# Attention and mixture of experts in one kernel: expert output moved beside the projections, halves made at projection, features regrouped by DMA

## The chip, the cores and the metric

The kernel runs on one core of a Trainium2 chip. The metric is the device time of one execution in microseconds. The time before is the median of three runs.

## The reference, cut to what matters

Input x is 4 x 1024 tokens of 256 values, all fp32. xn is the layernorm of x over its last dimension; the result is x + attention(xn) + experts(xn).

```
Q, K, V = (xn @ W.T).reshape(16, 4, 1024, 16)      # a plain reshape, not a transpose
scores  = einsum('hbqd,hbkd->hbqk', Q, K)
out     = einsum('hbqk,hbkd->hbqd', softmax(scores), V).reshape(b, s, -1)
y = out + xn;  attention = (y - mean(y)) / sqrt(var(y) + eps)      # over a whole batch entry
gates = two largest of xn @ w_gate.T (8 experts), softmax over the two
experts = sum over e of gates[:, e] * ((xn @ w_in[e].T) @ w_out[e].T)
```

The reshape cuts the 4096 tokens into 64 groups of 64 tokens (n = 0 to 63). Each group is one attention problem of 1024 positions of 16 values. As an expert has no nonlinearity, w_in[e].T @ w_out[e].T is first multiplied to one 256 x 256 matrix, its composite.

## The kernel before, in words

Products are made from fp32r values, which hold only the upper part of a number, so most operands are kept as two halves: hi, the cast value, and lo, the rest. A projection or an expert product is three products (hi x hi, hi x lo, lo x hi) summed in PSUM. The order on every engine is written out by hand, with semaphores between the engines; SP, ACT and POOL each run their lists in order. SP and ACT also issue the DMAs.

Stage one goes over eight chunks of 512 tokens (four tiles of 128). For chunk c, DVE and POOL make the layernorm (`layernorm`, L597 to L615), TensorE transposes it (L838), ACT copies hi (L456) and DVE makes lo (L626). TensorE projects query and key (`project_qk`, L849) and values with gate logits (`project_v`, L860), and makes the composite of expert c+1 in two halves of its weights (`expert_product`, L871); ACT and DVE cut the composite into halves (L446, L633). ACT copies query and key to `stage` and stores them to DRAM (`qk_d`), and values to `v_d`; the transposed halves go to DRAM as well (`xt_store`). SP loads x and, in two slots (`wp`), the weights (`load_weights`, L272, L274).

Stage two has two parts side by side. TensorE makes expert output tile by tile (`y_bank`, L907: four PSUM banks, each with two experts, six products each) from transposed halves that SP loads back from DRAM (`next_xt`), and DVE multiplies by the gates and adds (`add_experts`, L708, L710, L714). Meanwhile ACT loads query and key from `qk_d` regrouped to [16 values, 1024 positions] per group (`load_qk`, L518), casts hi (L525), POOL subtracts lo (L396), and ACT stores three rows of halves for queries and three for keys to `feat_d` (`split_qk`, L529).

The last eight tiles of 32 go beside the first sixteen turns of maxima: a turn is a block of 128 query positions of group 0 or 1 against 1024 keys (`max_scores`, L936) and its maximum on DVE (`maxima`, L725). In turn 10 the maxima of group 0 are transposed (`maxima_to_rows`, L980); they come through POOL (`max_halves`, L405, L407). SP puts them as two further rows into the query features (`max_rows`, L329).

The attention loop then goes over n: `scores` (L948, 50 rows: 48 of halves and two of the maximum), exponentials on ACT (`exps`, L557), the sum over values (L959) and, for group n+2, the maxima. SP loads the features of group n+4 (`features`, L314, four loads), values and maxima rows of group n+1. A normalisation over batch entries and the stores of the result end the kernel.

## Time and profile before

| | us |
|---|---|
| median of 3 runs (lowest, highest) | 1100.63 (1099.38, 1101.2) |
| profiled execution: time, span | 1102.04, 1100.2 |
| busy: TensorE matmul, VectorE | 999.7 (91%), 846.7 (77%) |
| busy: ScalarE, POOL | 648.6 (59%), 117.2 (11%) |
| mean granted TensorE clock | 0.96 of full |
| DMA | 133.59 MB in 115766 packets, 47328 of them under 512 B |

A profile is of one execution. The busy time of TensorE is that of its matmul row, in which pipelined products overlap, so a busy TensorE isn't one at its peak. A row gives the line of the kernel, the engine, the tiles (written <- read) and a duration. SPq and ACTq are DMA issues on those queues. The 40 slices are of 27.5 us each.

### The profile page before, as it was taken

Reading aid. Unit: us, or ns where it says so; the run is one execution under the profiler, and the core shown is the slowest. Engines: PE = TensorE matmul, PEld = TensorE weight load, DVE = VectorE, ACT = ScalarE, POOL = GpSimd, SP = SyncE. Lnnn points to the kernel's source line nnn. Section 1 sums busy time; section 2 is a strip of 40 time slices with the busy share of each in tenths; the row PEclk is TensorE's granted clock in tenths of the full one; section 3 lists DMA queues with packets and bytes.
Section 4 is the critical chain, followed back from the end, with each engine's and each line's share of the span. In section 5 each row is a group of like instructions: output and inputs, shape, how many; then the busy total and the mean of one; then the engine's idle time right before and its main releaser. Section 6 shows DMA issues by size and latency. Waiting matters only on the chain.

```text
span 1100.2 us, 21325 instructions
## 1 busy us (share of the span) xinstructions
PE 999.7 (91%) x7816; PEld 512.7 (47%) x7816; DVE 846.7 (77%) x1108; ACT 648.6 (59%) x1240; POOL 117.2 (11%) x221
## 2 busy tenths in 40 slices
PE   7999999999920699999999999999999999999995
PEld 6888878888710433333333333333333333333332
DVE  5333376767830479999999999999999999999976
ACT  3334310000000048888888888888888888888885
POOL 3221121011111100000000000000000000000001
PEclk9999999999965769999999999999999999999998
DMA  7999697679766512222223232322223232323214
GB/s 269 377 327 330 243 172 187 184 184 227 165 156 154 206 28 54 72 57 70 68 60 72 54 72 54 72 56 71 63 65 72 54 72 54 72 54 72 64 22 154
DMA packets 115766, 133.59 MB, mean 121 GB/s; under 512 B 47328, under 2 KB 84960, under 8 KB 115680
## 3 DMA queue, kind: packets, MB, share of 16 engines
q1 hardware_dynamic: 62560, 77.64, 27.2%
q10 hardware_dynamic: 53120, 54.80, 17.5%
q8 instruction: 55, 0.90, 0.4%
q14 instruction: 31, 0.25, 0.1%
HBM read 80.75 MB, written 50.59 MB: 119 GB/s over the span
## 4 chain that ended last, share of the span: by engine, by line
PE 69%; ACTq 9%; DMA 8%; ACT 5%; issue 5%; POOL 2%; DVE 1%; SPq 0%; POOLq 0%; DVEq 0%
PE ps L959 23%; PE ps L948 21%; PE ps L936 10%; DMA feat_d<-wp 8%; ACTq L529 5%; PE ps L871 4%; PE ps L849 4%; ACTq L518 4%; ACT wp L557 3%; PE ps L860 2%; PE ps L907 2%; PE ps L970 2%; ACT vstage L557 1%; PE ps L982 1%; POOL xnc L396 1%
## 5 line engine op out<-in xcount | busy, mean ns | idle before, releaser
L725 DVE TENSOR_REDUCE negm<-ps 128x1 f32<-128x1024 f32 x512 | 618.7, 1223 | 49.5 <-PE ps L936 40.7
L557 ACT ACTIVATE wp<-ps 128x512 f32<-128x512 f32 x684 | 374.0, 597 | 86.1 <-PE ps L948 62.6
L948 PE MATMUL ps<-qf,xth 50*128 50x512 f32 x1024 | 258.5, 499 | 23.3 <-ACT wp L557 13.8
L959 PE MATMUL ps<-wp,vb 128*17 128x256 f32 x2736 | 216.1, 388 | 0.1
L936 PE MATMUL ps<-xth,qf 48*128 48x512 f32 x1024 | 210.4, 403 | 0.3 <-DVE negm L725 0.3
L948 PEld LDWEIGHTS ps<-qf,xth 50*128 50x128 f32 x1024 | 98.3, 185 | 230.7 <-ACT wp L557 128.3
L557 ACT ACTIVATE vstage<-ps 128x512 f32<-128x512 f32 x170 | 101.7, 598 | 29.4 <-PE ps L948 17.8
L907 PE MATMUL ps<-mth,xtth 128*128 128x512 f32 x256 | 103.7, 405 | 1.0 <-ACT vstage L481 1.0
L936 PEld LDWEIGHTS ps<-xth,qf 48*128 48x128 f32 x1024 | 100.6, 190 | 8.5 <-issue 5.9
L959 PEld LDWEIGHTS ps<-wp,vb 128*17 128x17 f32 x2736 | 46.9, 95 | 118.6 <-ACT wp L557 46.1
L907 PE MATMUL ps<-mtl,xtth 128*128 128x512 f32 x256 | 101.8, 398 | 0.0
L907 PE MATMUL ps<-mth,xttl 128*128 128x512 f32 x256 | 101.8, 397 | 0.0
L557 ACT ACTIVATE picks<-ps 128x512 f32<-128x512 f32 x170 | 101.5, 597 | 0.0
L710 DVE SCALAR_TENSOR_TENSOR acc<-ps,gates,acc 128x256 f32 (+1 forms) x128 | 61.8, 483 | 43.3 <-PE ps L907 40.6
L525 ACT CAST wp<-stage 128x1024 fp32r<-128x1024 f32 x8 | 8.0, 1045 | 107.2 <-issue 107.2
L525 ACT CAST wp<-xnc 128x1024 fp32r<-128x1024 f32 x8 | 8.0, 1044 | 95.9 <-issue 95.9
L871 PE MATMUL ps<-wp 128*128 128x256 f32 x256 | 58.4, 387 | 5.7 <-DMA wp<-w_out_t 5.7
L907 PEld LDWEIGHTS ps<-mth,xtth 128*128 128x128 f32 x256 | 48.5, 189 | 15.9 <-issue 4.6
L405 POOL TENSOR_TENSOR mpart<-negm,zero 128x8 fp32r<-128x8 f32 x64 | 12.8, 200 | 402.1 <-DVE negm L725 402.1
L871 PEld LDWEIGHTS ps<-wp 128*128 128x128 f32 x256 | 49.1, 194 | 12.3 <-issue 5.7
L907 PEld LDWEIGHTS ps<-mth,xttl 128*128 128x128 f32 x256 | 48.5, 190 | 11.7
L959 PE MATMUL ps<-vstage,vb 128*17 128x256 f32 x680 | 53.7, 387 | 0.3 <-issue 0.2
(107 smaller groups left out, 775.8 us busy)
## 6 DMA issues: line engine op xcount, KB each, us to landing
qf<-feat_d SPq DMA_DIRECT2D x128, 192.0 KB, 3.4
feat_d<-wp ACTq DMA_DIRECT2D x32, 512.0 KB
xth<-feat_d SPq DMA_DIRECT2D x128, 96.0 KB, 3.4
wp<-w_in SPq DMA_DIRECT2D x16, 512.0 KB, 5.3
wp<-w_out_t SPq DMA_DIRECT2D x16, 512.0 KB, 6.3
qk_d<-stage ACTq DMA_DIRECT2D x8, 1024.0 KB, 5.1
v_d<-vstage ACTq DMA_DIRECT2D x8, 544.0 KB, 3.2
vb<-v_d SPq DMA_DIRECT2D x128, 34.0 KB, 2.1
```

Of the source, the lines that this page charges most:

```text
L518: act.dma_start(dqk[p][b * DH:(b + 1) * DH].rearrange("d (g t) -> d g t", t=TB), qk_d.rearrange("f (g d) t -> d (f g) t", d=DH) [:, :, bas ...
L529: act.dma_start(feat_d[f, bass.ds(c * BC, BC), r * DH:(r + 1) * DH, :], (hi[p][f].bitcast(FP32), dq[p][f])[part]).then_inc(feat_out[2 * p ...
L557: nc.scalar.activation(weight_tile(n, j, b)[:, h * HALF:(h + 1) * HALF], ps[:, ST_BANK[(2 * unit + b) % 3], :], ACT.Exp).then_inc(exp_done, 1)
L710: nc.vector.scalar_tensor_tensor(out=total, in0=product, scalar=gate, in1=total, op0=ALU.mult, op1=ALU.add).then_inc(ff_added[j], 1)
L725: nc.vector.tensor_reduce(negm[:, n % 2, qt:qt + 1], ps[:, b:b + 2, :].rearrange("p b c -> p (b c)"), AX.X, ALU.max, negate=True).then_inc ...
L849: last = nc.tensor.matmul(ps[:, QK_BANK[o], :], w[:, o // 2, kt, (o % 2) * P:(o % 2 + 1) * P], v[:, p, kt, :], start=i == 0, stop=i == len ...
L860: last = nc.tensor.matmul(ps[:, bank, 0:D + E], x_t[:, p, kt, t * P:(t + 1) * P], w[:, kt, :], start=i == 0, stop=i == len(products) - 1)
L871: last = nc.tensor.matmul(ps[:, M_BANK[dh], 0:D], win[s][:, h, dh * P:(dh + 1) * P], wout[s][:, h, :], start=s == 0 and h == 0, stop=s == ...
L907: last = nc.tensor.matmul(ps[:, Y_BANK[j], :], v[:, slot, kt, :], m[:, kt, 2 * j:2 * j + 2, :].rearrange("p e d -> p (e d)"), start=i == 0 ...
L936: last = nc.tensor.matmul(ps[:, MAX_BANK[turn % 2] + half, :], qf[rows, u, qt * P:(qt + 1) * P], kf[rows, u, :], start=True, stop=True)
L948: nc.tensor.matmul(ps[:, ST_BANK[(2 * unit + half) % 3], :], kf[rows, u, j * P:(j + 1) * P], qf[rows, u, h * HALF:(h + 1) * HALF], start=T ...
L959: last = nc.tensor.matmul(ps[32 * c:32 * c + VW, PV_BANK, 0:POS // 4], vb[:, n % 2, j + b * NKT // 2, :], weight_tile(n, j, b)[:, c * (POS ...
```

## The change

The order of the stages is changed and the query and key features take another way.

1. The composites of all eight experts are made first, beside chunk 0 alone. SP loads all weights through the same two slots and the eight chunks of x between them.
2. Then, for each chunk, TensorE makes the expert output of its four tiles directly from the transposed halves in SBUF, and between the tiles the transposes and projections of the next chunk. The store of the halves to DRAM and their loads go. The gate weights are computed chunk by chunk instead of once.
3. Query and key outputs are cut into halves when they leave PSUM: ACT copies hi, DVE subtracts to lo, and ACT stores each of four outputs of a chunk twice (eight stores of 256 KB on ACT's queue). `qk_d` now holds [16 column groups, query or key, hi or lo, 16, tokens].
4. `regroup`, eight DMAs a chunk on SP's queue, copies from `qk_d` to `feat_d` in DRAM, 256 KB each, in pieces of 64 tokens (256 B). `load_qk`, `split_qk` and POOL's split loop go. `feat_d` holds hi and lo once; `features` reads hi twice, in eight loads instead of four.
5. The last four tiles (before: eight) go beside the sixteen turns, one bank a turn. `kf` is a tile of its own, no longer laid over `xth`. Values and projections share two PSUM banks.

```diff
-    qk_d = nc.dram_tensor("qk_d", [2, KT * P, T], FP32, kind="Internal").ap()
-    feat_d = nc.dram_tensor("feat_d", [2, NB, FR, POS], FP32, kind="Internal").ap()
+    qk_d = nc.dram_tensor("qk_d", [G, 2, 2, DH, T], FP32, kind="Internal").ap()
+    feat_d = nc.dram_tensor("feat_d", [NB, 2, 2, DH, POS], FP32, kind="Internal").ap()
...
             for half in range(2):
                 first = half * ROWS
-                yield qf, slice(first, first + FR), slice(0, POS), feat_d[0, n]
-                yield kf, slice(first, first + FR), slice(0, HALF), feat_d[1, n, :, half * HALF:(half + 1) * HALF]
+                keys = slice(half * HALF, (half + 1) * HALF)
+                yield (qf, slice(first, first + 2 * DH), slice(0, POS),
+                       feat_d[n, 0, 0].unsqueeze(0).to_broadcast([2, DH, POS]))
+                yield qf, slice(first + 2 * DH, first + FR), slice(0, POS), feat_d[n, 0, 1]
+                yield kf, slice(first, first + 2 * DH), slice(0, HALF), feat_d[n, 1, :, :, keys]
+                yield kf, slice(first + 2 * DH, first + FR), slice(0, HALF), feat_d[n, 1, 0, :, keys]
...
+            def regroup(c):
+                for half in range(2):
+                    sp.wait_ge(qk_stored[half], 64 * (c + 1))
+                for n in range(BC * c, BC * (c + 1)):
+                    sp.dma_start(feat_d[n].rearrange("f h d (g t) -> (f h d) g t", t=TB),
+                                 qk_d[:, :, :, :, n * TB:(n + 1) * TB].rearrange("g f h d t -> (f h d) g t")
+                                 ).then_inc(regrouped[c], 16)
...
+            for e in range(1, E):
+                load_x(e)
                 for h in range(2):
-                    load_weights(2 * k - 1, h)
...
+                    load_weights(e, h)
...
+            regroup(0)
             sp.wait_ge(att_const, 2)
-            for f in range(2):
-                sp.wait_ge(feat_out[f], 48)
...
+            sp.wait_ge(regrouped[0], 16 * BC)
+            for n in range(SLOTS):
+                features(n)
+            sp.wait_ge(v_stored, 16)
+            values(0)
+            for c in range(1, NC):
+                regroup(c)
             sp.wait_ge(v_stored, 16 * NC)
-            values(0)
             max_rows(0)
...
                     for half in range(2):
                         sp.wait_ge(st_ready[half], NKT * (n + 1))
+                    if (n + SLOTS) % BC == 0:
+                        sp.wait_ge(regrouped[(n + SLOTS) // BC], 16 * BC)
                     features(n + SLOTS)
...
             def qk_out(c):
...
+                act.wait_ge(qk_stored[0], 64 * c)
                 for o in range(4):
...
+                    act.wait_ge(project_ready, 2 * TC * c + TC + o + 1)
+                    nc.scalar.copy(stage[:, o, :].bitcast(FP32R), ps[:, PROJECT_BANK[o % 2], :]).then_inc(qk_hi, 1)
+                    for half, (done, staged) in enumerate(((qk_hi, stage), (qk_lo, lo_stage))):
+                        act.wait_ge(done, 4 * c + o + 1)
+                        act.dma_start(qk_d[o % 2 * G // 2:(o % 2 + 1) * G // 2, o // 2, half, :, c * CH:(c + 1) * CH],
+                                      staged[:, o, :]).then_inc(qk_stored[half], 16)
...
+            for c in range(1, NC):
+                xt_out(c)
+                v_out(c)
+                second_weight(c)
                 qk_out(c)
...
+            def qk_lo_halves(c, outputs):
+                for half in range(2):
+                    dve.wait_ge(qk_stored[half], 64 * c)
+                for o in outputs:
+                    dve.wait_ge(qk_hi, 4 * c + o + 1)
+                    nc.vector.tensor_tensor(lo_stage[:, o, :], ps[:, PROJECT_BANK[o % 2], :], stage[:, o, :], ALU.subtract
+                                            ).then_inc(qk_lo, 1)
...
+            for c in range(NC - 1):
+                for i in range(TC):
+                    add_experts(TC * c + i, range(E // 2))
+                    if i == 0:
+                        lo_halves(c + 1)
+                    elif i == 1 and c + 2 < NC:
+                        layernorm(c + 2)
+                    elif i == 2:
+                        choose_experts(c + 1)
+                        qk_lo_halves(c + 1, range(2))
+                    elif i == 3:
+                        qk_lo_halves(c + 1, range(2, 4))
+                        gate_weights(c + 1)
+            for i in range(2 * NKT):
+                n, qt = divmod(i, NKT)
+                add_experts(NT - TC + i // 4, [i % 4])
...
                 maxima(n, qt)
...
+            for e in range(2, E):
+                for h in range(2):
+                    expert_product(e, h)
...
             pe.wait_ge(ml_done, KT * E)
...
+            for c in range(NC - 1):
+                for i in range(TC):
                     for j in range(E // 2):
-                        y_bank(XS * k + slot, slot, j)
+                        y_bank(TC * c + i, j)
+                    if i == 0:
+                        transposes(c + 1)
+                    elif i == 1:
+                        for t in range(TC):
+                            project_v(c + 1, t)
+                    else:
+                        for o in range(2 * i - 4, 2 * i - 2):
+                            project_qk(c + 1, o)
```

## Rows read from the trace of the kernel before

**Rows 1.** The page's 40 slices from 0: busy tenths, clock, GB/s

```profile
PE   7999999999920699999999999999999999999995
...
PEclk9999999999965769999999999999999999999998
...
GB/s 269 377 327 330 243 172 187 184 184 227 165 156 154 206 28 54 72 57 70 68 60 72 54 72 54 72 56 71 63 65 72 54 72 54 72 54 72 64 22 154
```

**Rows 2.** The page's chain of waits, shares of the span by line

```profile
PE ps L959 23%; PE ps L948 21%; PE ps L936 10%; DMA feat_d<-wp 8%; ACTq L529 5%; PE ps L871 4%; PE ps L849 4%; ACTq L518 4%; ACT wp L557 3%; PE ps L860 2%; PE ps L907 2%; PE ps L970 2%; ACT vstage L557 1%; PE ps L982 1%; POOL xnc L396 1%
```

**Rows 3.** The chain in order of time: start us, us, what

```profile
332.06 11.76 DMA feat_d<-wp
343.90 0.33 ACTq L518
```

**Rows 4.** Who waited for whom: us in total, times, longest us

```profile
PE ps L980 <- POOL mpart L407: 56.7, 1, 56.7
```

**Rows 5.** Timeline of TensorE: the first scores (start us, us, instruction)

```profile
391.05 0.69 PE L948 MATMUL ps<-qf,xth 50*128 50x512 f32 x2 [1.66 <-DVE ps L755]
```

**Rows 6.** Stretches: PE, PEld, DVE, ACT, POOL busy; clock, DMA share, GB/s

```profile
192.50:220.00 27.50, 27.50 (x119) 22.15 (x118) 19.75 (x45) 0.00 (x0) 1.44 (x1) 1.00 0.70 184
...
338.00:340.00 2.00, 0.00 (x0) 0.00 (x0) 0.00 (x0) 0.00 (x0) 0.00 (x0) 0.50 0.51 211
...
340.00:367.00 27.00, 0.00 (x0) 0.00 (x0) 0.00 (x0) 3.98 (x4) 9.53 (x6) 0.50 0.66 152
...
391.00:411.00 20.00, 19.14 (x97) 6.67 (x101) 13.23 (x13) 11.32 (x21) 0.80 (x4) 0.51 0.12 31
```

**Rows 7.** The chain in order of time, one chunk of stage one

```profile
33.92 5.58 PE ps L849 x24
39.49 1.47 PE ps L860 x12
40.96 0.87 PE ps L838 x8
...
43.30 6.91 PE ps L871 x32
```

**Rows 8.** DMA issues: count, KB each, median us to landing

```profile
wp<-w_out_t SPq DMA_DIRECT2D x16, 512.0 KB, 6.3
```

**Rows 9.** Timeline of VectorE in four stretches

```profile
17.12 1.39 DVE L597 BATCH_NORM_STATS2 st<-acc 128x6 f32<-128x256 f32 x4
...
20.75 1.38 DVE L615 TENSOR_SCALAR xnc<-acc,mean,rstd 128x256 f32<-128x256 f32 x4 [1.42 <-POOL rstd L381]
...
140.94 0.19 DVE L672 TENSOR_REDUCE top<-lg 128x4 f32<-128x32 f32 x1 [3.85 <-ACT lg L479]
...
143.41 0.19 DVE L685 TENSOR_TENSOR gap<-top 128x32 f32<-128x32 f32 x1
...
146.46 0.48 DVE L710 SCALAR_TENSOR_TENSOR acc<-ps,gates,acc 128x256 f32 x1 [0.39 <-DVE gates L692]
...
150.28 0.48 DVE L710 SCALAR_TENSOR_TENSOR acc<-ps,gates,acc 128x256 f32 x1
...
299.82 0.48 DVE L710 SCALAR_TENSOR_TENSOR acc<-ps,gates,acc 128x256 f32<-128x256 f32 x1 [0.17 <-PE ps L907]
...
301.84 0.49 DVE L710 SCALAR_TENSOR_TENSOR acc<-ps,gates,acc 128x256 f32<-128x256 f32 x1
```

**Rows 10.** Groups of instructions: busy us, mean ns of one, idle before

```profile
L469 ACT COPY stage<-ps 128x512 f32<-128x512 f32 x32 | 18.8, 587 | 27.6 <-PE ps L849 27.6
```

**Rows 11.** Timeline of SP's DMA issues in the attention loop

```profile
602.80 0.42 SPq L314 DMA_DIRECT2D xth<-feat_d  x1
607.20 1.18 SPq L319 DMA_DIRECT2D vb<-v_d  x2
```

**Rows 12.** DMA from 150 to 157 us, while qk_d's pieces are loaded

```profile
DMA packets 3723, 1.06 MB, mean 152 GB/s; under 512 B 3165, under 2 KB 3723, under 8 KB 3723
...
q10 hardware_dynamic: 3133, 0.78, 97.7%
```

More of the change, by code:

```diff
@@ L522, in split_qk @@
-            def split_qk(c, p, gen):
-                act.wait_ge(dq_in[p], 16 * BC * (gen + 1))
-                for f in range(2):
-                    nc.scalar.copy(hi[p][f], dq[p][f]).then_inc(hi_done[f], 1)
-                for f in range(2):
-                    act.wait_ge(lo_done[f], c + 1)
-                    for r, part in enumerate(((0, 0, 1), (0, 1, 0))[f]):
-                        act.dma_start(feat_d[f, bass.ds(c * BC, BC), r * DH:(r + 1) * DH, :],
-                                      (hi[p][f].bitcast(FP32), dq[p][f])[part]).then_inc(feat_out[2 * p + f], 16)
@@ L676, in pick, with choose_experts @@
                 g(nc.vector.tensor_tensor(onehot[:, rows], eq[:, rows], wide(first[:, rows]), ALU.is_equal))
-            for chunks, rows in ((NC - 1, slice(0, NT - TC)), (NC, slice(NT - TC, NT))):
-                for h in range(2):
-                    dve.wait_ge(lg_evac[h], 2 * chunks)
+            def choose_experts(c):
+                rows = slice(TC * c, TC * (c + 1))
+                dve.wait_ge(v_evac, 2 * TC * (c + 1))
                 pick(rows, lg, top1, oh1)
@@ L853, in project_v, with project_qk @@
-            def project_v(c, p, t):
-                bank = V_BANK[t % 2]
-                pe.wait_ge(v_evac[t % 2], 2 * c + t // 2)
-                pe.wait_ge(lg_evac[t % 2], 2 * c + t // 2)
+                    last.then_inc(xt_psum, 1)
+            def project_qk(c, o):
+                p = c % 2
+                if o < 2:
+                    pe.wait_ge(v_evac, 2 * (TC * c + o + 3))
+                else:
+                    pe.wait_ge(qk_lo, 4 * c + o - 1)
+                products = [(w, v, kt) for w, v in ((wqkh, xth), (wqkh, xtl), (wqkl, xth)) for kt in range(KT)]
+                for i, (w, v, kt) in enumerate(products):
+                    last = nc.tensor.matmul(ps[:, PROJECT_BANK[o % 2], :], w[:, o // 2, kt, (o % 2) * P:(o % 2 + 1) * P],
+                                            v[:, p, kt, :], start=i == 0, stop=i == len(products) - 1)
+                last.then_inc(project_ready, 1)
@@ L858, in project_v @@
+            def project_v(c, t):
+                p = c % 2
+                if t == 0:
+                    pe.wait_ge(xtl_done, KT * (c + 1))
+                if t >= 2:
+                    pe.wait_ge(v_evac, 2 * (TC * c + t - 1))
+                elif c:
+                    pe.wait_ge(qk_lo, 4 * (c - 1) + t + 3)
                 products = [(x_t, w, kt) for kt in range(KT) for x_t, w in ((xth, wvgh), (xth, wvgl), (xtl, wvgh))]
                 for i, (x_t, w, kt) in enumerate(products):
-                    last = nc.tensor.matmul(ps[:, bank, 0:D + E], x_t[:, p, kt, t * P:(t + 1) * P], w[:, kt, :],
+                    last = nc.tensor.matmul(ps[:, PROJECT_BANK[t % 2], 0:D + E], x_t[:, p, kt, t * P:(t + 1) * P], w[:, kt, :],
```

390 lines of the change are left out of this document (128 added, 262 removed).

## The prediction, before the changed kernel ran

> **What bounds the kernel now.** I read the 40 slices first [rows 1]. TensorE works in nearly all of them, except from slice 11 to 13, some 302 to 385 us, where it stands still and its clock falls. The chain of waits [rows 2] gives 8% of the span to the stores of the features and 9% to the DMA issues of the two lines around them (L529 and L518). In order of time [rows 3] a chunk of this work ends with the last of its six stores, issued at 332.06 and landed 11.76 us later, and only then are the loads of the next but one issued (343.90). Eight chunks run so, one behind the other, from the end of the projections to 367. The waits name the place where this is paid: TensorE's L980 (`maxima_to_rows`) stood for 56.7 us behind `mpart` [rows 4], whose POOL instruction stands behind the last subtraction of the split loop. So the order is: projections beside the experts' products to about 142 us, 24 token tiles of expert output and ten attention turns to 310 us, an idle hole to 367, six more turns, and the first scores at 391.05 [rows 5]. In the hole the granted clock is 0.50 of full (1.2 GHz) [rows 6]. After 391 everything is the attention loop, 709.2 us long.
>
> The profiled execution took 1102.04 us with a span of 1100.2, 1.84 around it. The median shown is 1100.63, 1.4 below that execution. I make the sum against the span and take the same distances.
>
> **Removed.** The 64 loads of `qk_d` into SBUF, 16 ScalarE casts, 16 POOL subtractions and 48 feature stores go, and with them the hole: 56.7 us. The round trip of x's halves through DRAM (16 stores, 64 loads) goes too; it was hidden behind TensorE, so it is worth nothing by itself.
>
> **First phase, composites alone.** Before, an expert's two halves (32 products, 6.91 us) lay between 9.4 us of other TensorE work, so that a chunk took 16.3 us and weights were in time [rows 7]. Now six experts follow each other with two weight slots. A slot's cycle is: 3.45 us of products (half of 6.91), two issues about 0.4 us apart, 6.3 us to landing of the second load [rows 8], some 0.3 us of semaphores: 10.5 us for an expert, where TensorE needs 6.9. Bandwidth isn't the limit (2.6 MB in 10.5 us is 250 GB/s, the slices reach 377). I start from before's first stretch, which is the same to 17 us (VectorE is at its second layernorm at 17.12 [rows 9]); these steps are estimates from the products' durations in [rows 7]: `project_v(0)` and expert 1's first half to 24, its second half, whose weights are asked for at 17, to 28. The four query and key outputs come next at ScalarE's pace, because for each it copies (0.59 [rows 10]), waits for VectorE's half (about as long) and issues two stores (0.42 each, as SP's in [rows 11]): some 2 us an output, to 36. Expert 2 to 43, experts 3 to 7 at 10.5: 95.5. TensorE stands for 3.5 us in each cycle, and a stand of 1.7 us ahead of the first scores was already followed by 20 us at 0.51 [rows 5, 6]. I charge 1.3 us for each of five restarts, and 1 for the last subtraction: **the chunks begin at 103 us**. The bounds: 85 if loads land in 4.5 us, 118 if every restart costs a half product at the low clock.
>
> **Seven chunks.** TensorE: four tiles of expert output, 24 products each; 119 products in 27.5 us [rows 6] are 0.231 each, so 5.55 a tile, 22.2 together; query and key 5.58, values 2 x 1.47, transposes 0.87 [rows 7]: 31.6 us. VectorE: four tiles at 3.8 us when nothing holds it up (146.46 to 150.28), a layernorm of 5.0 (17.12 to 22.13), twelve steps of the expert choice at 0.225 (140.94 to 143.41), gate weights about 1.4, `lo_halves` 1.3, query and key halves 2.6 [rows 9]: 28.2 us. So TensorE sets the pace, with 3.4 us to spare for VectorE. VectorE also waits on ScalarE's hi copies, whose next copy stands behind two store issues: some 2 us. I stepped through one chunk: VectorE is furthest behind at the chunk's end, 3.7 us after TensorE, and has caught up in the second tile. The four banks of the output always come free in time. I take 32.2 us, seven times is 225: **328 us**. ScalarE is busy some 12 us of the 32 with copies and issues and is no bound. POOL's one copy of `xn` a chunk (2 us) can block a sum of two SBUF operands, and falls in the same slack.
>
> **Sixteen turns with the last four tiles.** Each now has one bank and one maximum: VectorE takes 2.02 (299.82 to 301.84) [rows 9] and 0.5 more once a tile, TensorE 1.39 + 0.43. VectorE bounds: 34.3 us, plus the 3.7 by which it begins late and 0.7 for memset and first rows. Before, the corresponding sixteen turns held two banks at 3.42. `mpart` is free on POOL now, so no hole. **First scores at 367 us**, instead of 391.05 [rows 5]: 24 us earlier.
>
> **The attention loop.** Same engine work, 709.2 us. SP issues eight feature loads instead of four, with the same bytes: +4 x 0.46 = 1.9 us, in a stretch from 603.22 to 607.20 in which it only waits [rows 11], so nothing; without this cover `max_rows`, next in its queue, would start late and scores(n+1) wait for it. The load of query's two equal copies has a source whose outermost dimension is 2. The feature stores, with an outermost dimension of 8, kept 0.51 of the sixteen engines busy at 211 GB/s [rows 6], 26 GB/s for each of eight. If such a shape sets how many engines serve, two serve each copy: 128 KB take 2.5 us, twice per n: 5 us, over before `max_rows` is issued some 7 us after the first of the features. Cost 0, and up to 0.5 us per n if it is more (d). The 8 us that the low clock cost from 391 to 411 I leave in: it may go (-8) or stay.
>
> **The queues, the cost with no row.** `regroup` moves 8192 pieces of 256 B a chunk from DRAM to DRAM on SP's queue. Nearest row: 3723 packets, nearly all of 256 B, in 7 us with the engines full [rows 12]: 16 x 7 us / 3723 = 30 ns each. That is a read into SBUF; here the write is short too. From below 30 ns or 15.4 us a chunk, from above twice that, 31 us, each side paid in full. I take 35 ns (18 us), nearer the row, as reads and writes overlap. The split stores of query and key (outermost 8: half the engines, 2 MB at 211 GB/s) add 10 us on those engines and values 2: 30 us in a chunk of 32. It hides, and features are wanted only from n = 4 on. But `max_rows(0)` stands behind all eight regroups.
>
> **Sum.** 367 + 709.2 + 1.8 = 1078 for such an execution, 1.4 less for the median: **1076.6 us**, a gain of 24: 56.7 of hole and about 3 of low clock after it, less some 30 for weights and restarts, less 5 for VectorE's lateness.
>
> **Rivals.**
> (a) *Regroup backs up; slower.* `max_rows(0)` must land before 367. Regroups start at about 92; each of seven chunks costs the busier engines 512 packets plus 12 us, the last 512 packets alone: 92 + 84 + 4096 t = 367 gives t = 46 ns. Below that nothing; at 60 ns the last lands at 422, scores(0) waits 55 us and the median is 1131. For: the engines are near full already and short writes are new; the chain of before shows such pieces as slow. Against: 30 ns measured. The Trainium skill ("DMA: Bandwidth & Descriptors", "Specifications") states that transfers below 512 B make the engine read, modify and write; no row here shows a short write to DRAM, and by the Trainium skill alone this rival would win. Chance 17%.
> (b) *VectorE sets the chunk.* If its waits on ScalarE and POOL's port cost 7 us a chunk instead of 3, a chunk is 35.5: +23 us, 1100, no change. For: 28 of 32 us busy and a queue in strict order; against: each wait was stepped through. 8%.
> (c) *The low clock stays through the composites.* A half then takes 6.9 instead of 3.45, a slot's cycle 14; six times 3.5, less the 6.5 charged, is 14.5 us, up to 20 if loads are late too: median 1091 to 1097, still faster. For: every cycle has its stand; against: the products before it raised the clock each time. 15%.
> (d) *Two-engine loads hold up `max_rows` in every n.* If the key copies run on two engines as well, 8 us of each 10.5 are taken; 0.5 us per n times 60 is 30 us: 1107. For: 0.51 of the engines in [rows 6]; against: the key copies lie in DRAM with one step and may count as 32 rows. The Trainium skill ("DMA: Bandwidth & Descriptors", the rules for kernel authors, "Use all 16 engines") states that a leading broadcast of c copies confines a DMA to at most c engines; the share in [rows 6] agrees for 8, and by the Trainium skill two engines carry the query copies for certain. Chance 5%.
> (e) *No low clock at the start of attention and quick weights*: 1060. 12%. The forecast itself has 43%.
>
> **Numbers.** A measurement of this kernel tells 0.2%, 2.2 us. Faster: forecast, (c) and (e), with part of (b): 0.74. Same 0.05. Slower: (a), (d), a little of (b): 0.21. The range runs from 1058 to 1116, with part of (a)'s middle and all of (b) to (e); the likeliest case alone is 1068 to 1086.
>
> **What would show it.** The first tile of expert output at 103; chunks of 32.2 with TensorE at 9 throughout; the slices from 0 to 100 us with TensorE at 6 or 7 and perhaps a clock below 10; no wait of L980 on `mpart`; first scores at 367; 709 us from there. Wrong would be: TensorE waiting for `ff_added` or `qk_lo` in the chunks (b), a long wait of the first scores with DMA full to that point (a), a DMA wait of the scores in every n (d), `qf<-feat_d` landing in over 10 us.

## The result, and the profile after

The changed kernel takes **1067.18 us** (median of four runs, 1065.44 to 1068.25), the kernel before in the same session 1100.51: a ratio of 0.9697 with a 95% interval of 0.968 to 0.9714, 33 us faster. Forecast were 1076.6 us in a range of 1058 to 1116, so the sign and the range held and the middle was 9.4 us too high. The profiled execution took 1067.98 us, 0.8 above the median, with a span of 1066.2.

The page's slices come first, then its line of packets and its chain of waits:

```profile
PE   7778999999999899999999999999999999999995
...
PEclk9899999999999799999999999999999999999998
DMA  7777455644555022222222222222222222222204
...
DMA packets 127042, 108.58 MB, mean 102 GB/s; under 512 B 81120, under 2 KB 102368, under 8 KB 126944
...
PE ps L885 23%; PE ps L874 20%; PE ps L829 15%; PE ps L862 10%; PE ps L801 4%; PE ps L775 3%; DMA wp<-w_out_t 3%; ACT wp L464 3%; PE ps L790 2%; PE ps L896 2%; DVE negm L620 2%; ACT vstage L464 1%; PE ps L908 1%; DVE acc L608 1%; PE ps L763 1%
```

Against [rows 1] the hole of slices 11 to 13 is gone. Against [rows 2] no feature store and no line of ScalarE's issues is in the chain; what DMA still holds are weight loads of the composites, 3%. The slices 0 to 3 (of 26.7 us each) are the new weak place, with TensorE at 7 or 8. The waits of TensorE name it (engine, line, waited for: us in total, times, longest):

```profile
PE ps L801 <- DMA wp<-w_out_t: 22.8, 7, 7.7
...
PE ps L829 <- DVE spare L552: 2.4, 1, 2.4
PE ps L874 <- DVE ps L679: 1.7, 1, 1.7
PE ps L829 <- DVE mtl L542: 0.9, 1, 0.9
```

The wait of 56.7 us behind `mpart` [rows 4] has no successor. In its place stand 22.8 us for weights, of which 7.7 is the very first wait of the program. The rest lies in the composites, shown in TensorE's timeline (start us, us, instruction, idle before it; the last row is the start of the last four tiles):

```profile
47.94 10.05 PE L801 MATMUL ps<-wp 128*128 128x256 f32 x32 [5.79 <-DMA wp<-w_out_t]
59.67 7.14 PE L801 MATMUL ps<-wp 128*128 128x256 f32 x32 [1.68 <-DMA wp<-w_out_t]
68.94 7.14 PE L801 MATMUL ps<-wp 128*128 128x256 f32 x32 [2.12 <-DMA wp<-w_out_t]
78.74 3.69 PE L801 MATMUL ps<-wp 128*128 128x256 f32 x16 [2.65 <-DMA wp<-w_out_t]
82.90 3.72 PE L801 MATMUL ps<-wp 128*128 128x256 f32 x16 [0.47 <-DMA wp<-w_out_t]
88.98 7.39 PE L801 MATMUL ps<-wp 128*128 128x256 f32 x32 [2.36 <-DMA wp<-w_out_t]
97.29 0.50 PE L829 MATMUL ps<-mth,xth 128*128 128x512 f32 x1 [0.92 <-DVE mtl L542]
...
323.12 0.50 PE L829 MATMUL ps<-mth,xth 128*128 128x512 f32 x1 [2.44 <-DVE spare L552]
```

Expert 3 stands 5.79 us for its weights and then needs 10.05 us for what the others do in 7.14. The chain in order of time gives the landing of the weights it stood for, and of those of expert 4 behind it (start us, us):

```profile
39.10 8.70 DMA wp<-w_out_t
...
54.95 4.59 DMA wp<-w_out_t
```

The stretches (PE, PEld, DVE, ACT, POOL busy; clock, DMA share, GB/s) show what went on beside them, and give the other stages:

```profile
42.00:48.00 6.00, 0.21 (x2) 0.09 (x1) 2.13 (x6) 0.37 (x1) 2.17 (x2) 0.92 1.00 366
47.00:53.80 6.80, 5.86 (x14) 4.72 (x15) 0.00 (x0) 0.00 (x0) 0.00 (x0) 0.50 0.46 175
53.80:97.00 43.20, 33.29 (x148) 27.11 (x146) 4.01 (x10) 3.72 (x10) 0.00 (x0) 1.00 0.83 262
129.20:161.00 31.80, 31.80 (x153) 26.36 (x152) 25.18 (x75) 5.29 (x15) 3.11 (x3) 1.00 0.56 159
323.49:326.90 3.41, 3.41 (x9) 2.03 (x8) 1.68 (x7) 0.00 (x0) 0.00 (x0) 0.50 0.51 154
325.00:359.00 34.00, 32.05 (x125) 19.07 (x124) 32.36 (x54) 0.00 (x0) 0.41 (x2) 0.97 0.34 81
...
359.12:379.12 20.00, 18.86 (x116) 6.75 (x118) 15.24 (x14) 12.69 (x24) 0.81 (x4) 0.66 0.09 28
```

While expert 3's weights were awaited, the DMA engines were full (share 1.00, 366 GB/s). From 38 to 48 us ScalarE's queue, with the stores of chunk 0's query and key halves, moved 1.28 MB beside the 2.06 MB of SP's queue; from 54 to 60 us, when expert 4's weights came, it moved nothing. So the stores are the likely reason for 8.70 us against 4.59, though no run took them away. After the stand of 5.79 us the granted clock was 0.50 (1.2 GHz) for 6.8 us; after the composites' stands of 1.68 to 2.65 us it stayed at 1.00. But a stand of 2.44 us ahead of the last four tiles, where TensorE waits for VectorE's halves of query and key, was followed by 3.4 us at 0.50. So the length of a stand alone doesn't tell whether the clock falls. In a chunk TensorE is busy 31.80 of 31.80 us. In the tail (325 to 359) it is VectorE that is full, 32.36 of 34. Chunks and first scores follow from TensorE's timeline too:

```profile
166.65 1.03 PE L763 MATMUL ps<-ident,xnc 128*128 128x128 f32 x8
198.58 1.03 PE L763 MATMUL ps<-ident,xnc 128*128 128x128 f32 x8
```

One transpose follows the other by 31.93 us, and the distance is 31.84 to 31.93 in every chunk. The scores' first product starts at 359.12 (391.05 before [rows 5]) and the attention loop, from there to the end of the span, is 707.1 us. The regroups, as SP issues them, and their landing (the page's DMA issues: count, KB each, median us):

```profile
87.57 10.05 SPq L266 DMA_DIRECT2D feat_d<-qk_d  x8
```

```profile
feat_d<-qk_d SPq DMA_DIRECT2D x64, 256.0 KB, 4.4
...
wp<-w_in SPq DMA_DIRECT2D x16, 512.0 KB, 4.0
wp<-w_out_t SPq DMA_DIRECT2D x16, 512.0 KB, 5.6
```

So SP spends some 1.25 us on one regroup of 1024 pieces, and half of them land within 4.4 us. By the durations of single packets in the trace a piece of 256 B took 18 ns on its engine, where I had put 35; a packet of 4096 B took 159 ns.

### The profile page after: what moved, and what is told of

Read it like the earlier page. It is cut to its first block, busy times and chain, and to the rows that moved or that the text cites. A ratio compares the mean times of both kernels' runs of the same rounds, so it can differ in the third digit from the quotient of the medians.

```text
span 1066.2 us, 20587 instructions
## 1 busy us (share of the span) xinstructions
PE 1003.2 (94%) x7816; PEld 513.4 (48%) x7816; DVE 873.2 (82%) x1255; ACT 634.4 (60%) x1231; POOL 78.4 (7%) x205
## 3 DMA queue, kind: packets, MB, share of 16 engines
q8 instruction: 62, 1.02, 0.4%
## 4 chain that ended last, share of the span: by engine, by line
PE 82%; ACT 5%; issue 5%; DVE 4%; DMA 3%; ACTq 0%; SPq 0%; POOL 0%; POOLq 0%; DVEq 0%
PE ps L885 23%; PE ps L874 20%; PE ps L829 15%; PE ps L862 10%; PE ps L801 4%; PE ps L775 3%; DMA wp<-w_out_t 3%; ACT wp L464 3%; PE ps L790 2%; PE ps L896 2%; DVE negm L620 2%; ACT vstage L464 1%; PE ps L908 1%; DVE acc L608 1%; PE ps L763 1%
## 5 line engine op out<-in xcount | busy, mean ns | idle before, releaser
L874 PE MATMUL ps<-qf,kf 50*128 50x512 f32 x1024 | 257.7, 498 | 23.6 <-ACT wp L464 14.1
L862 PE MATMUL ps<-kf,qf 48*128 48x512 f32 x1024 | 209.7, 401 | 0.4 <-DVE negm L620 0.4
L874 PEld LDWEIGHTS ps<-qf,kf 50*128 50x128 f32 x1024 | 97.9, 184 | 229.8 <-ACT wp L464 127.4
L829 PE MATMUL ps<-mth,xth 128*128 128x512 f32 x256 | 103.8, 405 | 3.4 <-DVE spare L552 2.4
L862 PEld LDWEIGHTS ps<-kf,qf 48*128 48x128 f32 x1024 | 99.9, 188 | 9.0 <-issue 5.7
L829 PE MATMUL ps<-mth,xtl 128*128 128x512 f32 x256 | 101.4, 396 | 0.0
L829 PE MATMUL ps<-mtl,xth 128*128 128x512 f32 x256 | 101.4, 396 | 0.0
L801 PE MATMUL ps<-wp 128*128 128x256 f32 x256 | 63.2, 407 | 22.8 <-DMA wp<-w_out_t 22.8
L608 DVE SCALAR_TENSOR_TENSOR acc<-ps,gates,acc 128x256 f32<-128x256 f32 x128 | 61.1, 478 | 18.3 <-PE ps L829 17.6
L829 PEld LDWEIGHTS ps<-mtl,xth 128*128 128x128 f32 x256 | 48.5, 189 | 10.1
L885 PE MATMUL ps<-picks,vb 128*17 128x256 f32 x680 | 53.2, 385 | 0.0
```

The source lines that it names most:

```text
L608: nc.vector.scalar_tensor_tensor(out=total, in0=product, scalar=gate, in1=total, op0=ALU.mult, op1=ALU.add).then_inc(ff_added[j], 1)
L801: last = nc.tensor.matmul(ps[:, M_BANK[dh], 0:D], win[s][:, h, dh * P:(dh + 1) * P], wout[s][:, h, :], start=s == 0 and h == 0, stop=s == ...
L829: last = nc.tensor.matmul(ps[:, Y_BANK[j], :], v[:, p, kt, tokens], m[:, kt, 2 * j:2 * j + 2, :].rearrange("p e d -> p (e d)"), start=i == ...
L862: last = nc.tensor.matmul(ps[:, MAX_BANK[turn % 2] + half, :], qf[rows, u, qt * P:(qt + 1) * P], kf[rows, u, :], start=True, stop=True)
L874: nc.tensor.matmul(ps[:, ST_BANK[(2 * unit + half) % 3], :], kf[rows, u, j * P:(j + 1) * P], qf[rows, u, h * HALF:(h + 1) * HALF], start=T ...
L885: last = nc.tensor.matmul(ps[32 * c:32 * c + VW, PV_BANK, 0:POS // 4], vb[:, n % 2, j + b * NKT // 2, :], weight_tile(n, j, b)[:, c * (POS ...
```

## The experiments

The kernel before had a median of 1100.1 to 1101.2 us beside each group of runs. "First tile" is the start of the first tile of expert output, "loop" the time from the first scores to the end of the span; both are read from one profiled execution. The first tile came at 97.29 in the changed kernel and at 93.43 to 96.65 in the four others whose first phase is the same (experiments 1, 2, 5 and 7), so a difference of 4 us in it need be no effect of an edit.

**1. Twice the regroups.** Each regroup is made a second time into DRAM that nobody reads.

```diff
+                    for again in again_d:
+                        sp.dma_start(again[n]..., qk_d[..., n * TB:(n + 1) * TB]...).then_inc(again_s, 16)
```

> The changed kernel with every regroup DMA issued twice, the second time into a DRAM tensor that nobody reads. Theory: regrouping is far from its limit. The changed kernel's profile has eight issues of one chunk in 10.05 us, and a chunk of 31.84 us has the DMA engines 0.56 busy; twice the pieces make about 20 us of SP's queue a chunk, still under 31.84, so first scores stay at 359 us and the time within 0.3% of the changed kernel's 1067.2 (1064 to 1070). Rival (a) of the prediction: the engines are near full; then SP's max_rows(0) is late by 10 to 60 us and the time is 1077 to 1127, with a wait of the first scores.

Measured: 1066.63 us (1065.28 to 1067.29), ratio 0.969 (0.9642 to 0.9738), first scores 358.27. The doubled traffic costs nothing: rival (a) is out at twice its load, not only at its own.

**2. Four times the regroups.** The same edit with three copies, to find the limit.

> Every regroup is made four times (three of them into DRAM that nobody reads), all on SP's queue. In the changed kernel a 256 B packet of the regroup takes 18 ns on its engine and one issue of 1024 pieces takes SP 1.25 us. Theory (it is SP's issuing that ends first, bandwidth second): 32 issues a chunk x 1.25 = 40 us where a chunk lasts 31.9, so the issues fall behind by some 8 us in each of seven chunks; the last regroup comes 60 to 90 us late, max_rows(0) and the features behind it as well, and the first scores move from 359.1 to 410 to 450: median 1110 to 1160. Rival 1 (the cost is hidden at any size): 1067 +- 2, first scores 359. Rival 2 (packets of 18 ns in parallel with all other traffic decide: 2048 x 18 ns = 37 us a chunk on each engine beside 12 us of other traffic): the same order of delay, but then SP's issue instructions get longer than 1.25 us each, or the regroup's landing grows beyond 50 us.

Measured: 1200.49 us, ratio 1.0909 (1.0865 to 1.0954), slower than the kernel before. TensorE's waits and two stretches of this kernel:

```profile
PE ps L881 <- DMA qf<-ot: 133.5, 1, 133.5
```

```profile
350.00:400.00 50.00, 7.13 (x29) 4.08 (x27) 9.56 (x16) 0.00 (x0) 0.41 (x2) 0.61 1.01 230
400.00:480.00 80.00, 0.00 (x0) 0.00 (x0) 0.00 (x0) 0.00 (x0) 0.00 (x0) 0.50 1.03 234
```

The one wait is what rival (a) described: the first scores stand for row maxima whose issue is behind all the regroups, until 490.6. Its place and form were right; its price was not. The second row also says what a piece costs: with nothing beside them the DMA engines are full (1.03) and move 234 GB/s, so 256 KB take 1.12 us, or 16 x 1.12 / 1024 = 17.5 ns a piece. SP's rows of this stretch (start us, us, line, count):

```profile
469.98 3.32 SPq L272 DMA_DIRECT2D again_d<-qk_d  x3
473.34 1.15 SPq L268 DMA_DIRECT2D feat_d<-qk_d  x1
```

Four issues take 4.55 us, 1.14 each, so here SP issues without a pause while the engines are full. The run doesn't tell which of the two is the limit. The signs named for the second rival didn't come as such: the median issue lasted 1.02 and 1.12 us on the two lines, not more than 1.25, and the landings had medians of 4.5 and 4.6 us with a longest of 20.7, not 50. Single issues did last up to 10.4 us. The time expected (1110 to 1160, first scores at 410 to 450) was too small by 40 us.

**3. Four weight slots.** Two of them lie in a tile that is not yet in use; every load is asked for one expert earlier.

```diff
-                if e:
-                    sp.wait_ge(*((m_ready, KT * e) if s else (half_done, e)))
+                if e > 1:
+                    sp.wait_ge(*((m_ready, KT * (e - 1)) if s else (half_done, e - 1)))
```

> The changed kernel with four slots for the experts' weights instead of two (the other two lie in xn's last sixteen tiles, which are written only later). Theory: the composites are bound by the cycle of a slot (wait for the product, issue, 5.6 us to landing), for which TensorE stood about 16 us and ran one expert at the low clock (10.05 us instead of 7.1). With four slots the stands fall to what the DMA rate leaves: 2.62 MB an expert at 350 to 377 GB/s is 7.0 to 7.5 us against 6.9 of products, plus about 1 us an expert until the halves of the last composite are cut. First tile of expert output at 84 to 88 us instead of 97.3, time 1054 to 1058. Rival: the DMA rate sets the phase in the changed kernel too; then the first tile stays within 3 us of 97.3 and the time within 3 us of 1067.

Measured: 1056.53 us (1052.61 to 1059.06), ratio 0.9604 (0.9554 to 0.9654), 10.6 us faster than the changed kernel; first tile at 85.19. Its waits and one of the experts in the timeline:

```profile
PE ps L805 <- DMA wp<-w_out_t: 8.0, 1, 8.0
PE ps L805 <- DVE mtl L545: 6.3, 5, 2.6
```

```profile
52.81 7.17 PE L805 MATMUL ps<-wp 128*128 128x256 f32 x32 [0.92 <-DVE mtl L545]
60.91 7.17 PE L805 MATMUL ps<-xn 128*128 128x256 f32 x32 [0.92 <-DVE mtl L545]
```

The time and the first tile are as expected. All weight waits but the program's first are gone, and so is the low clock of 47 to 54. What is late next is the accumulator's bank: 2.6 us once and 0.92 for each expert behind it, until ScalarE has copied and VectorE subtracted. The profile is of the shortest of the four executions (1052.61 us).

**4. The kernel before with POOL's order changed.** POOL makes the first `mpart` after the split of chunk 4 instead of behind the last.

```diff
+            for c in range(5):
+                split_lo(c)
...
             max_halves(0)
+            for c in range(5, NC):
+                split_lo(c)
```

> The kernel before, with one reordering on POOL: the halves of group 0's maxima are made after the split of chunk 4 instead of after chunk 7, so that L980 no longer stands behind the split loop. Theory: the hole belongs to ScalarE's chain of loads, casts and stores that ends near 372 us; POOL's wait is only where it is seen. Then TensorE finishes its turns by about 335, stands instead at the first scores because ScalarE comes to its first exponential only at 373 to 384, and of the 57 us of hole only 8 to 18 are gained: 1083 to 1093. Rival: the POOL queue is the cause; then the hole closes, 45 to 57 us are gained: 1044 to 1056, better than the changed kernel.

Measured: 1097.0 us (1094.06 to 1099.64), ratio 0.996 (0.9934 to 0.9986). TensorE, in order of time:

```profile
332.76 0.50 PE L953 MATMUL ps<-qf,xth 50*128 50x512 f32 x2 [1.65 <-DVE ps L760]
...
388.63 0.79 PE L953 MATMUL ps<-qf,xth 50*128 50x512 f32 x2 [55.14 <-ACT wp L562]
```

The first scores come 58 us earlier and the second wait 55.14 us: the hole only moved. ScalarE's own row shows what it was doing:

```profile
387.98 1.08 ACT L562 ACTIVATE wp<-ps 128x512 f32<-128x512 f32 x2 [23.61 <-DMA feat_d<-wp]
```

Its exponentials stand behind the feature stores in its queue. So the 56.7 us that [rows 4] put under POOL are the length of the chain of loads, casts and stores of [rows 3]; POOL was only where they were seen first. The change gains because it removes that chain. The expected 1083 to 1093 was not reached.

**5. Query's copies in two loads.** The load with a leading dimension of two is split, so that each has 16 rows outermost.

```diff
-                yield (qf, slice(first, first + 2 * DH), slice(0, POS),
-                       feat_d[n, 0, 0].unsqueeze(0).to_broadcast([2, DH, POS]))
+                for copy in range(2):
+                    yield qf, slice(first + copy * DH, first + (copy + 1) * DH), slice(0, POS), feat_d[n, 0, 0]
```

> The changed kernel with the load of query's two equal copies made as two loads of 16 rows each, whose outermost dimension is 16 on both sides. Theory: the broadcast load runs on two engines but has time, so nothing changes: within 0.2% of the changed kernel's 1067.2, the attention loop (first scores to the end) 707 us in both; landing of the loads of qf from feat_d falls to 2 to 3.5 us. Rival (d): two-engine loads cost something in every n; then the attention loop gets 5 to 30 us shorter. Second rival: SP's two further issues per n make it late; then the loop is longer by more than 2 us.

Measured: 1066.23 us (1061.57 to 1068.59), ratio 0.9692 (0.9641 to 0.9742), the same as the changed kernel. No wait of the scores on a DMA stands in the changed kernel's list, so rival (d) is out. The expected landing of 2 to 3.5 us was met (2.2). The times don't say how many engines serve such a load, but the landing records in the packed traces do. On each of the four semaphores that count feature loads, the changed kernel has 1632 landings for 16 groups, 102 a group, and this one 2560, 160 a group, which is 16 for each of its ten loads. All loads but query's hi copies are the same in both, so each of those two has 3 landings and the key copies have 16. ScalarE's stores with an outermost dimension of 8 have 9 each (288 for 32). That fits two engines, sixteen and eight, if one record more is counted where fewer than sixteen serve; so the key copies did not run on two engines, as (d) supposed.

**6. Banks and the order of x.** Four slots, two pairs of accumulator banks used in turn, x's chunks 2 to 7 loaded after the weights.

```diff
-        M_BANK = (4, 7)
+        M_BANK = ((4, 7), (5, 6))
...
-                if s == 0 and e:
-                    pe.wait_ge(ml_done, KT * e)
+                if s == 0 and e > 1:
+                    pe.wait_ge(ml_done, KT * (e - 1))
```

> Four weight slots, x's chunks 2 to 7 asked for after all weights, and the two accumulators of an expert in other banks for odd experts, so that expert e waits for the split of expert e-2 and not of e-1. With four slots alone the first tile of expert output came at 85.19 and TensorE still stood 6.3 us in five waits for the composites' low halves (mtl). Theory (each expert's 1 us between m_ready, ScalarE's copy and VectorE's subtraction is the bank's price): those waits go, first tile at 79 to 81, first scores near 340, median 1050 to 1052. Rival (the weights are then late, since six experts of 2.1 MB come at no more than 370 GB/s, 5.7 us each, beside stores): a wait of TensorE on DMA takes their place, first tile at 84 to 86, median 1055 to 1058.

Measured: 1047.24 us (1046.57 to 1049.22), ratio 0.9508 (0.9474 to 0.9542), first tile at 77.7, first scores at 338.14. TensorE's timeline:

```profile
35.16 7.07 PE L808 MATMUL ps<-wp 128*128 128x256 f32 x32
42.06 7.07 PE L808 MATMUL ps<-xn 128*128 128x256 f32 x32
48.97 7.07 PE L808 MATMUL ps<-wp 128*128 128x256 f32 x32
```

An expert every 6.91 us, with no stand: the 6.91 of [rows 7] is reached, and the composites are TensorE's. That is better than expected (first tile at 79 to 81, 1050 to 1052 us), and the rival's late weights did not come. Against the changed kernel the first tile is 19.6 us earlier and the median 19.9. Slots, banks and the order of x were not tried one by one beyond experiment 3.

**7. Early turns.** The sixteen attention turns that share the tail with the last four tiles go into chunks 1 to 6, three in each, on the transposes' banks. The schedule in short:

```diff
+                    if early_turn(c, i):
+                        pe.wait_ge(xtl_done, KT * (c + 2))
+                        max_scores(*early_turn(c, i))
```

> The changed kernel with the sixteen turns of groups 0 and 1 moved into chunks 1 to 6 (three a chunk, on the two banks of the transposes), so that the last four tiles of expert output stand alone. In the changed kernel these sixteen turns with four tiles are set by VectorE, 34 us from 325 to 359; VectorE has about 4 us to spare in each chunk and a maximum costs it some 1.1 us, three of them 3.3; TensorE's turn costs 0.43. Theory: chunks get 0.9 us longer for TensorE's three turns (6 x 1.3 = 8 us in all), the tail shrinks from 34 to about 22 (four tiles at 5.55), so the first scores come at 353 to 355 and the median is 1060 to 1063. Rival (VectorE then sets the chunk): six chunks at 34.5 to 35, first scores at 360 to 366, median 1068 to 1074.

Measured: 1068.98 us (1065.84 to 1070.24), ratio 0.9706 (0.9672 to 0.974): nothing gained. A chunk's stretch, and TensorE's transposes:

```profile
134.00:167.50 33.50, 33.50 (x158) 26.53 (x157) 26.83 (x74) 5.00 (x16) 3.12 (x3) 1.00 0.52 143
```

```profile
233.96 1.03 PE L772 MATMUL ps<-ident,xnc 128*128 128x128 f32 x8
...
267.92 1.03 PE L772 MATMUL ps<-ident,xnc 128*128 128x128 f32 x8
```

A chunk lasts 33.96 us, 2.1 more than 31.87, and TensorE is full in it: three turns cost it 0.7 each and not the 0.43 that I had. Six chunks with them give back 10 us (301.87 against 294.18 at the last transposes, from a start 2.5 earlier). The tail, from there to the first scores, is shorter by 10.3 (54.7 against 64.9). VectorE had the room, as the theory said and the rival denied; the price was TensorE's. The time lies in the rival's range (1068 to 1074), but not for the rival's reason.

**8. All of it together.** Experiments 6 and 7 in one kernel.

> Four weight slots, x late, two pairs of accumulator banks, and the early turns, all in the changed kernel. Theory (the two gains lie in separate stretches and add): the gain of the slots and banks run over the changed kernel plus that of the early turns run, about 16 + 6 us, median 1043 to 1047. Rival (the earlier start takes away what hid the regroups or VectorE's lateness): above 1050.

Measured: 1048.74 us (1046.46 to 1049.96), ratio 0.9513 (0.9478 to 0.9548), like experiment 6 alone, which fits a gain of nothing from the turns. The expected 1043 to 1047 assumed their 6 us; the rival's "above 1050" did not come either.

**9. The round trip of x put back.** The halves are stored and loaded again, into a tile that nobody reads, in the changed kernel.

```diff
+            def xt_store(c):
+                act.wait_ge(xtl_done, KT * (c + 1))
+                for half, dst in ((xth, xth_d), (xtl, xtl_d)):
+                    act.dma_start(dst[:, :, c * CH:(c + 1) * CH]..., half[:, c % 2]...).then_inc(xt_stored[c], 16)
```

> The changed kernel with a round trip of x's two halves through DRAM put back: two stores of 512 KB per chunk (256 KB per half and kt) from ScalarE's queue once both halves are made, and two loads of the same bytes on SP's queue into a tile that nobody reads, ahead of each regroup. Theory (the round trip that the change removed was hidden, so its removal was worth nothing): 1067 +- 2 us, first scores at 359 +- 1, chunks of 31.9. Rival (the queues' extra waits hold ScalarE's query and key copies, the banks of the projections come free late and a chunk grows by about 1 us): 1073 to 1076, first scores 365 to 368.

Measured: 1066.03 us (1065.28 to 1066.99), ratio 0.9668 (0.9623 to 0.9714). The saved traffic was worth nothing by itself, as forecast; 16 MB more through the same queues don't show in the time, and a chunk still lasts 31.9 us. The first scores came at 354.7 and not at 358 to 360, 3.0 us of it by a first tile at 94.3; the loop was 709.7 us long, the last section says why.

**10. The stand ahead of the first scores filled.** To experiment 6, eight products of 512 columns are added whose result nobody reads.

```diff
+            for _ in range(8):
+                nc.tensor.matmul(ps[:, MAX_BANK[...], :], mth[:, 0, 0, 0:P], xth[:, (NC - 1) % 2, 0, :],
+                                 start=True, stop=True)
```

> The kernel with four slots, x late and two pairs of banks (1047 us, first scores at 338.14, attention loop 707.6 of which 13.65 us at a granted clock of 0.50, beginning some 2 us after a stand of 1.72 us), with eight products of 512 columns into a bank that is free put in this stand. Theory (the stand ahead of the first scores brings the low clock): the granted clock stays 1.00 from 338 to 355, the loop takes 701 to 702, median 1041 to 1042. Rival (the low clock comes from the first steps of the loop, in which TensorE waits for the exponentials at every product pair, and not from the stand): the same stretch of 0.50 within 3 us, loop 707, median 1046 to 1048.

Measured: 1044.85 us (1043.2 to 1051.42), ratio 0.9483 (0.9443 to 0.9522), between the two expectations.

**11. The first steps of the loop filled as well.** After each of the first four score steps, eight products of 128 columns more.

> The same, and eight products of 128 columns more after each of the first four score steps, while no sums of values run yet (they cover most of TensorE's stands of 0.4 us there). If the stand and the sparse first steps both count: no low clock, loop 701 to 703, median 1041 to 1043, also where the kernel with the stand alone filled keeps its low stretch. Rival (neither counts; the change of kind of product or something else lowers the clock): low stretch of 13.65 us as before, 1047 to 1050, since the fillers then only add their own time.

Measured: 1044.44 us (1044.07 to 1045.08), ratio 0.9473 (0.9439 to 0.9506). The two medians are the same, the spreads are not: 8 us of experiment 10 against 1 us here. The first 20 us of the loop, in the kernel before [rows 6] 0.51 and in the changed one 0.66, are here, for experiment 6, 10 and 11 in this order:

```profile
338.14:358.14 20.00, 18.86 (x116) 6.68 (x118) 15.17 (x14) 12.62 (x24) 0.81 (x4) 0.66 0.11 27
```

```profile
337.40:357.40 20.00, 18.49 (x104) 6.26 (x105) 13.87 (x13) 11.94 (x22) 0.81 (x4) 0.61 0.11 30
```

```profile
338.18:358.18 20.00, 19.68 (x173) 9.74 (x172) 17.10 (x16) 15.29 (x29) 0.81 (x4) 1.00 0.12 35
```

In the profiled execution of experiment 10 the low clock still comes, later and for 17.1 us, so something besides this stand can bring it. But that execution, of 1048.56 us, is the second longest of its six. The mean granted clock over the whole span, which every execution has, tells of the rest: in experiment 10 it was 0.994, 0.993, 0.994 and 0.994 in four executions of 1043.2 to 1045.8 us, and 0.988 and 0.986 in those of 1048.56 and 1051.42 us. In experiment 6 it was 0.986 to 0.990 in all four, in experiment 11 0.995 in all six, where the only low stretch of the trace is the last 9.6 us of the span. By an estimate from these means (7 to 10 us at the end of every trace here are low too), 0.993 and 0.994 leave 2 to 9 us at the low level at the start of the loop, where experiment 6 has 10 us or more.

So the stand likely matters: filled alone, it left little of the low clock in four of six executions, against none of four in experiment 6, which was timed in another session. With the first steps filled as well, in which TensorE otherwise stands about 0.4 us ahead of each pair of scores for ScalarE's exponentials, it came in none of six. What the steps do alone is not shown, as they were not filled without the stand. The loop is 709.3 us in the second row's execution and 704.6 in the third's, fillers included. What they cost is seen in the starts of the first scores in TensorE's timeline, of experiment 6 and then of experiment 11:

```profile
338.14 0.50 PE L881 MATMUL ps<-qf,kf 50*128 50x512 f32 x2 [1.72 <-DVE ps L685]
...
339.29 0.50 PE L881 MATMUL ps<-qf,kf 50*128 50x512 f32 x2 [0.42 <-ACT wp L470]
```

```profile
338.18 0.50 PE L881 MATMUL ps<-qf,kf 50*128 50x512 f32 x2
...
338.85 1.11 PE L952 MATMUL ps<-xth,mth 128*128 128x128 f32 x8
339.88 0.50 PE L881 MATMUL ps<-qf,kf 50*128 50x512 f32 x2
```

A step takes 1.70 us with them and 1.15 without, 2.2 us in four steps. The gain over experiment 6, 2.8 us of medians in another session, lies within the intervals and is not shown by them. With experiment 10 this is the fastest version run: 5.3% below the kernel before, 2.1% below the changed one.

## Why the prediction was right, and where it was off

**The hole.** Right, and experiment 4 shows it from the other side: the chain of stores had to go, the order of POOL's work alone is worth 3 to 4 us.

**First phase: 103 predicted, 97.3 measured; the largest part of the error.** The form was right (two slots, TensorE standing in every cycle; experiment 3 removes the stands with the slots). The terms were off in both directions, so 5.7 us is a difference of larger errors. A cycle was put at 10.5 us, with 6.3 from issue to landing, and a restart at 1.3. The median landing after is 5.6, and experts 4 to 7 took 38.4 us together (57.99 to 96.37), 9.6 each, without a low clock: 8.8 us less than the four times 11.8 charged. Expert 3 took 15.8 us (from 42.15 to 57.99), 4.0 more than charged, 2.9 of it by the low clock (10.05 - 7.14). The step that failed for it is "bandwidth isn't the limit": 250 GB/s is the mean of a cycle's loads and leaves out the 2 MB of query and key stores of chunk 0, and the engines were full (366 GB/s, share 1.00) when its weights were wanted. Expert 2 ended at 42.15, where 43 was said. Rival (c), a low clock through all the composites, is out.

**Seven chunks: 32.2 predicted, 31.9 measured.** Right. TensorE full, VectorE at 25.2 of 31.8 us instead of 28.2; rival (b) is out. From the first tile, seven chunks end at 97.3 + 223 = 320, where 328 was said.

**Sixteen turns: 39 predicted, 39 measured** (320 to 359.1), with VectorE the bound as said. Its lateness at the end of the last chunk is seen as TensorE's stand of 2.44 us. Experiment 7 shows that moving them helps nobody while TensorE is full in the chunks.

**First scores:** 367 predicted, 359.1 measured, 5.7 of it from the first phase and 2.2 from the chunks.

**Attention loop: 709.2 predicted, 707.1 measured.** I had left the low clock's 8 us in, "it may go or stay"; a part went. Nothing shows that this part is an effect of the change; it is rather luck of the two executions: the low stretch is 20.5 us long in the one and 13.7 in the other, and by the last section the clock differs as much between executions of one kernel. Eight feature loads instead of four cost nothing (experiment 5 has ten). Rival (e) asked for no low clock at the start and quick weights; neither came with the change.

**The regroup: 35 ns a piece predicted, 17.5 to 18 measured.** The term that failed is the lower bound: it was taken from pieces read into SBUF, full engines, 30 ns [rows 12], and DRAM to DRAM was cheaper than that, not dearer. It changed no time, but it sized rival (a), whose 17% was too much: the point from which it decides was put at 46 ns, and even twice the load is hidden. Four times the load is not: experiment 2 gives 1200 us. Nor is the chain of before a sign for (a), as was said ("shows such pieces as slow"): the stores of [rows 3] go in packets of 4096 B by the trace. The Trainium skill ("DMA: Bandwidth & Descriptors", "Specifications") says that transfers under 512 B don't reach the line rate and are read, modified and written. The rate agrees: with full engines the 256 B pieces moved at 234 GB/s (experiment 2) and packets of mostly 1 to 4 KB at 366 (42 to 48 us above). That reading, modifying and writing is the reason, no run here shows, as these packets also go another way (SBUF to or from DRAM). The price was far too small for (a) to win by.

**Sum.** 9.4 us of error: 5.7 first phase, 2.2 chunks, 2.1 the clock in the loop, less 0.6 because the median stood 0.8 and not 1.4 below the profiled execution. The last two terms are of single executions.

## What to carry to other kernels

When a stage is moved to a place where it stands alone, look at what covered its loads before: here the composites gained stands of some 15 us that no one saw while other TensorE work lay between them, and slots and banks gave 20 us back. A wait that the profile puts under one engine may be the length of a chain in another engine's queue; advance only the waiting part, and if the hole moves on, it is the chain. Moving work from a stage bound by one engine into a stage where that engine has room gains nothing if the other engine, full there, has a part in it.

## What had not been expected of the hardware

The low granted clock at the start of the attention loop varies in length between executions, and the loop with it. The first three columns are of the profiled execution, the last is the mean granted clock over the whole span of every execution timed:

| kernel | low stretch, us | clock in the loop's first 20 us | loop, us | clock of all executions |
|---|---|---|---|---|
| before | 20.5 | 0.50 | 709.2 | 0.954 to 0.966 |
| x's round trip put back | 20.5 | 0.54 | 709.7 | 0.983 to 0.987 |
| stand filled | 17.1 | 0.61 | 709.3 | 0.986 to 0.994 |
| changed | 13.7 | 0.66 | 707.1 | 0.985 to 0.987 |
| four slots and banks | 13.7 | 0.66 | 707.5 | 0.986 to 0.990 |
| early turns | 13.7 | 0.66 | 707.4 | 0.982 to 0.988 |
| both of these | 13.7 | 0.66 | 707.2 | 0.988 to 0.991 |
| twice the regroups | 10.2 | 0.74 | 705.2 | 0.983 to 0.987 |
| four slots | 10.2 | 0.74 | 705.3 | 0.986 to 0.992 |
| ten feature loads | 6.8 | 0.83 | 704.3 | 0.984 to 0.989 |
| stand and first steps filled | none | 1.00 | 704.6, fillers included | 0.995 |

The rows are not a ranking of the kernels. The loop's instructions are the same in most of them, and executions of one kernel differ as much: 0.001 of mean clock in a span of 1050 us is 2.1 us at the low level, so 0.986 to 0.992 with four slots are some 13 us (the means don't say at which place). The profiled execution of the kernel with ten feature loads is the shortest of its four (1061.57 us; the others took 1065.21 to 1068.59 at a mean clock of 0.984 to 0.986), and so is that with four slots. What sets the length was not found; filling the stand and the first steps is the only edit here that took it away in every execution. Without the fillers' 2.2 us the last row's loop would be 702.4, an estimate, so 20.5 us at the low level were worth about 7 us of the kernel before (8 in the forecast). So a difference of a few us between two profiles should be looked up in this stretch before it is put down to an edit, and the mean clock of the other executions is the check.
